# GpSimd's product waits for the LSTM's h of its slot, and the scan's step moves up to stand directly behind the LSTM's step

## The reference

```
def step(h, inp):                  # Mamba
    h = dA * h + d_t[..., None] * b_t[:, None, :] * u_t[..., None]
    y = jnp.einsum('bds,bs->bd', h, c_t)
def step(carry, xg_t):             # LSTM
    g = xg_t + h @ W_hh.T
    c = sigmoid(f) * c + sigmoid(i) * tanh(gg)
    h = sigmoid(o) * tanh(c)
```

## Time and profile before

| | |
|---|---|
| median of 3 runs | 3049.94 us (3046.9 to 3051.22) |
| the profiled execution: time, span | 3049.58 us, 3047.8 us |
| mean granted TensorE clock | 0.829 |
| busy: TensorE, VectorE, ScalarE, GpSimd | 82%, 62%, 45%, 33% |
| scans, weighings, products of drive in all | 256 each |

### The profile page before, as it was taken

One profiled execution on the slowest core, in us unless ns is written; L12 is line 12 of the kernel. 1 busy time (PEld: TensorE's weight loads), 2 busy tenths in 40 slices (PEclk: granted clock), 3 DMA queues, 4 the chain that ended last, 5 costly groups with the idle time before them and its releaser, 6 DMA issues.

```text
span 3047.8 us, 31113 instructions
## 1 busy us (share of the span) xinstructions
PE 2512.8 (82%) x7376; PEld 1272.4 (42%) x7376; DVE 1891.7 (62%) x6562; ACT 1384.6 (45%) x4624; POOL 1014.8 (33%) x913
## 2 busy tenths in 40 slices
PE   5677864489987999799978999699979996899698
PEld 1223442254444444444434444444444445444444
DVE  5575885467766777577756876677755555444322
ACT  3323333345544554455544554455534444444233
POOL 4343464135432564244523653245520002000200
PEclk8797556579995999689987999699968996898589
DMA  3232331023220332122311321123201210121021
GB/s 121 84 85 72 114 101 39 0 59 100 73 84 16 103 101 67 29 82 80 108 46 44 106 82 60 37 73 111 80 12 65 69 56 11 42 70 56 6 81 59
DMA packets 111776, 204.74 MB, mean 67 GB/s; under 512 B 14799, under 2 KB 24422, under 8 KB 111592
## 3 DMA queue, kind: packets, MB, share of 16 engines
q1 hardware_dynamic: 111592, 202.75, 22.1%
HBM read 195.36 MB, written 7.34 MB: 67 GB/s over the span
## 4 chain that ended last, share of the span: by engine, by line
PE 41%; DVE 32%; ACT 12%; issue 8%; POOL 1%; DVEq 0%; POOLq 0%; ACTq 0%
PE p_hid L651 9%; DVE state L1215 7%; PE p_turn L912 6%; ACT cell_t L926 4%; PE p_misc L668 4%; DVE cell L942 3%; DVE add_c L939 3%; DVE weighed L1224 3%; PE p_acc L668 3%; DVE p_turn L936 2%; DVE terms L828 2%; PE p_gate L465 2%; DVE hist L947 2%; PE p_hid L962 2%; PE p_up L469 1%
## 5 line engine op out<-in xcount | busy, mean ns | idle before, releaser
L912 PEld LDWEIGHTS p_turn<-hist,w_hh 22*128 22x128 f32 x2048 | 366.6, 222 | 1027.6 <-DVE hist L947 887.9
L912 PE MATMUL p_turn<-hist,w_hh 22*128 22x4 f32 x2048 | 452.2, 289 | 344.7 <-DVE hist L947 327.1
L651 PE MATMUL p_hid<-xhat,w 128*128 128x512 f32 x1024 | 580.9, 650 | 8.0 <-DVE xhat L381 7.2
L926 ACT ACTIVATE cell_t<-cell 20x4 f32<-20x4 f32 x1024 | 207.7, 203 | 679.8 <-DVE cell L942 679.8
L1142 POOL TENSOR_TENSOR drive<-du,rows 128x512 f32<-128x512 f32 x256 | 453.9, 1773 | 66.8 <-DVE p_turn L1215 28.5
L712 ACT ACTIVATE hid<-p_hid,b1f 128x512 f32<-128x512 f32 x512 | 351.8, 687 | 262.8 <-PE p_misc L668 141.2
L936 DVE SCALAR_TENSOR_TENSOR p_turn<-p_turn,cell 20x4 f32<-20x4 f32 x1024 | 170.7, 167 | 459.3 <-ACT p_turn L922 435.7
L388 POOL TENSOR_TENSOR n_rstd<-n_var,minus_half 128x4 f32<-128x4 f32 x56 | 61.7, 1103 | 1076.1 <-DVE n_var L376 1076.1
L1161 POOL TENSOR_TENSOR y<-y,weighed 128x512 f32<-128x512 f32 x192 | 242.4, 1263 | 411.1 <-DVE weighed L1224 410.4
L947 DVE SCALAR_TENSOR_TENSOR hist<-p_turn,cell_t 20x4 f32<-20x4 f32 x1024 | 162.6, 159 | 275.6 <-ACT cell_t L926 275.6
L922 ACT ACTIVATE p_turn<-p_turn 96x4 f32<-96x4 f32 x1024 | 157.9, 154 | 374.1 <-PE p_turn L912 371.3
(11 more groups left out here) (220 smaller groups left out, 3404.3 us busy)
## 6 DMA issues: line engine op xcount, KB each, us to landing
rows<-rows_dram SPq DMA_DIRECT2D x128, 512.0 KB, 5.1
w<-w_dram SPq DMA_DIRECT2D x128, 256.0 KB, 2.7
w<-in_w2T SPq DMA_DIRECT2D x128, 256.0 KB, 2.7
comb_b<-comb_dram SPq DMA_DIRECT2D x64, 512.0 KB, 4.6
rows<-comb_dram SPq DMA_DIRECT2D x128, 128.0 KB, 2.9
w<-in_w1T SPq DMA_DIRECT2D x16, 256.0 KB, 2.7
w_dram<-w SPq DMA_DIRECT2D x16, 256.0 KB, 2.1
out_xT<-result SPq DMA_DIRECT2D x8, 256.0 KB, 2.5
```

The lines of the kernel that those rows point to most:

```text
L651: nc.tensor.matmul(p_hid[:, v % 2, :], w1[:, v // FB, (v % FB) * P:(v % FB + 1) * P], xhat[:, :], start=True, stop=True).then_inc(g_h, 1)
L912: nc.tensor.matmul(gate_bank(i)[:, :, t:t + 1], w_hh[:, :], before, start=False, stop=False, skip_group_check=True).then_inc(gates_done, 1)
L926: nc.scalar.activation(cell_t[64:64 + PE_, :], cell[32:32 + PE_, :], ACT.Tanh, scale=0.5).then_inc(cell_tanh, 1)
```

## The change

`put_drive` gets an argument `step`. Where it is not zero, GpSimd waits before the product until h of the slot in which the product stands has been written. In `period` the scan's step (with the bursts of decays that go with it in period 0) is taken from the end of the slot and put behind the LSTM's step, ahead of `layer1`, `layer0`, `fold` and `soft`, on all engines. Which slots move the scan on is the same. Products outside a period (in `opening`) and the first product of a chunk (at the end of `soft`) keep `step` 0.

```
-    def put_drive(u, k):
+    def put_drive(u, k, step=0):
...
         if n >= 2:
             pool.wait_ge(scan_done, n - 1)
+        if step:
+            pool.wait_ge(h_done, step)
         nc.gpsimd.tensor_tensor(flat(drive[:, n % 2, :, :]), du[:, j, :], rows[:, (u * S + s_) % ROWS, 0, :], ALU.mult).then_inc(driven, 1)
...
+    step_now = {"h": 0}
...
-                put_drive(u, k + 1)
+                put_drive(u, k + 1, step_now["h"])
...
             next(lstm, None)
+            step_now["h"] = i * CH + slot + 1 if i < NCH and slot < CH else 0
...
+            wide = 0
+            heavy = layer1 is not None and slot >= att and 6 <= o < LAYER - 1 and slot < tail
+            if u < NCH and heavy and soft[1] > SOFT:
+                advance(scan, "scan", SCAN)
+            if u < NCH and layer1 is None and soft[1] > SOFT:
+                if done["scan"] == 0:
+                    for _ in range(6):
+                        next(burst, None)
+                elif done["scan"] % 2 == 0:
+                    next(burst, None)
+                if done["scan"] <= SCAN:
+                    advance(scan, "scan", SCAN)
             if layer1:
                 next(layer1, None)
-            wide = 0
-            heavy = layer1 is not None and slot >= att and 6 <= o < LAYER - 1 and slot < tail
...
-                elif layer1 is None:
-                    if done["scan"] == 0:
-                        for _ in range(6):
-                            next(burst, None)
-                    elif done["scan"] % 2 == 0:
-                        next(burst, None)
-                    if done["scan"] <= SCAN:
-                        advance(scan, "scan", SCAN)
-                elif heavy:
-                    advance(scan, "scan", SCAN)
```

## The result

| | before | after |
|---|---|---|
| median (lowest to highest), 4 runs each on one chip | 3050.58 us (3046.9 to 3051.95) | 3017.8 us (3012.74 to 3025.97) |
| the profiled execution: time, span | 3049.58, 3047.8 | 3012.74, 3010.9 |
| mean granted TensorE clock | 0.829 | 0.831 |

A forecast was written before the change was run, and what follows sets the result against it. The LSTM chain from h to h was taken as the bound, set by TensorE in heavy slots without a scan and DVE with one. Gains of 30 (periods 1 to 5) plus 3 (period 0) gave 3016.5 us, range 3003 to 3035.

The forecast's parts named there:

- the main term: Periods 1 to 5: 160 scans fall from 1.429 to 1.22 us, 33 us, less 3 for three late scans.
- the 0.37 us gap: Unexplained DVE idle time before three scans, letting the product in first; these stay late, 3 x 1.0 = 3 us.
- The margin of the race: Scan slots: scan starts 0.19 us after h, the waiting product 0.24, so the scan leads by 0.05.
- rival A: Scan slots: the product wins against the scan, slots about 3.23 us, +123 us, about 3173; chance 0.08.
- the hidden heads: Early part of scan (0.15 us) and product (0.19) before each asks for its inputs, putting the product about 0.09 behind.
- In a weighing slot DVE's sum stays: Weighing slots: weighing of 0.68 us with L841 or L828 after it instead of ahead, DVE's total unchanged.
- Rival B: Handovers cost: addition to y overlaps the next scan, or product's tail delays the weighing; 3023.5 to 3036; chance 0.15 for 3027 to 3042.
- Period 0: Scans gain 8 us, L1344 meeting the addition to y gives back 6; gain taken as 3, between loss 4 and gain 11.
- the clock: A changed granted TensorE clock, listed among the signs that the forecast was wrong; no size given.
- C: Counted delays are replaced one for one, for instance in light slots between layers; 3050 us; chance 0.03.
- D: Period 0 gives its 11 us and light slots gain from the product that left; 3005 or less; chance 0.04.

The follow-up runs named there:

- e1: Kernel before plus only GpSimd's wait for h ahead of the product, slot order as before: 3034.65 us, ratio 0.994.
- e2: Kernel before plus only the new order, scan's step moved ahead, without the wait for h: 3073.99 us, ratio 1.0075.
- e8: Kernel after plus a one-column DVE copy from PSUM partition 0 ahead of the weighing in `terms` slots, periods 1 to 5: 3034.71 us.
- e10: Kernel after plus 10 one-column DVE writes to an unused tile in the first LSTM step of period 6: 3030.52 us.
- e11: Kernel after plus 40 one-column DVE writes to an unused tile in the first LSTM step of period 6: 3037.93 us.
- e7: Kernel after, but in period 0 weighing steps go back behind `layer0` and `fold`, scan steps staying in front: 3020.96 us, ratio 0.9916.
- e6: Kernel after with period 0 put back to the old order and no wait: 3019.12 us, ratio 0.9913.
- after: The changed kernel itself, as first measured against the kernel before: 3017.8 us, ratio 0.9898.
- e3: The kernel after run once more, unchanged, against the kernel before: 3018.56 us, ratio 0.9879.
- e9: Kernel after, but only DVE's queue has the new order, other engines the old one: 3035.81 us, ratio 0.9945.
- e5: The ladder: kernel after plus small DVE writes before each scan, none in periods 0 and 1, up to four in period 5: 3115.81 us.

## Why the prediction was right, and where it was not

**The cause and the main term were right.** The scan was long because of GpSimd's operation ahead of it, either the product (slots of 3.2) or the addition to y (1.39). The sum put this at 33 us less 3; the scans gave 29.9 and the scan slots 32.1. Scan slots are 2.25, but for three of 3.51 behind the 0.37 us gap, exactly as many as were taken out of the sum. `e1` and `e2` show that both parts are needed: by the medians, alone they give -15 and +24 us, and in the scan slots of periods 1 to 5 alone -11 and +14, together -32.

**The margin of the race was mis-sized, harmlessly.** I took 0.08 us from DVE's end to GpSimd's start, from the weighing and the addition to y. From the end of L947 to the waiting product it is 0.16 to 0.17 (1331.59 + 0.16, 1331.91). The product was to start 0.24 behind its L947 and starts 0.33 behind it. The margin is 0.13 to 0.14, not 0.05, so rival A was further off than I thought. On the other hand the hidden heads on which I leaned are no protection: the ladder turns when the starts are equal. Had the signal taken 0.08, the scan would by the ladder still have won, with 0.05 to spare and no more.

**"In a weighing slot DVE's sum stays" is the step that failed.** Two DVE operations do not take the same time in both orders. `terms` behind the weighing begins 0.03 after its end, and the weighing behind `terms` began 0.08 before its end (the slot of before shown above). That is 0.11 to 0.12 a slot, in 60 `terms` slots 7 us, most of the 9 that weighing slots lost. `e8` shows the cause. The order in the earlier trace rows held the overlap (1346.92 + 0.69 against 1347.53), so a term for "who overlaps whom" could have been read there; for `terms` in the second place no row showed it.

**Rival B in its own form did not come.** The addition to y reaches 0.10 into the scan (forecast 0.05) and the product 0.03 into the weighing (1331.91 + 2.15, against 1334.03); the scan takes 1.23 and the weighing 0.69. Those hundredths are all that this overlap costs. (The 3036 that rival B names for all of its losses together does not come out of its own terms: 3016.5 + 7 + 8 + 3 is 3034.5.)

**Period 0 had, on average, the wrong sign.** Forecast -3; measured +1.6 to +4.9 between the two profiles of each kernel, and +2.4 between the means of all profiles with the same code in this stage, whose ranges overlap slightly (316.6 to 320.0 against 314.7 to 316.9). In the groups by line above the scans gave 7.5 of the forecast 8, and L1344 and L548 together took 6.5 where 6 were forecast (2.0 and 4.5). What the sum left out is the same 0.11 as with `terms`: in 20 slots L558 or L563 now begins 0.03 behind the end of a scan or a weighing, where that scan or weighing used to begin 0.08 ahead of their end. That is 2 us, and I had counted a gain in just those slots. How the rest divides is not measured.

**The total was right partly by luck.** In the profiles of the first table, against a forecast of -33 stand -26 to -27 in periods 1 to 5, +2 to +5 in period 0, -8 to -10 in periods 6 and 7 and -1 to -6 in the opening. Without the last two the kernel would be faster by some 21 to 25 us. With `e10` and `e11` counted, whose code in periods 1 to 5 is the same, the gain there is 20 to 27. What the last two stages gave is not the work of the change as such: `e7` and `e10` carry the change in periods 1 to 5, and their periods 6 and 7 took 590.8 and 590.7, as long as in the kernel before. `e6`, which has the change in periods 1 to 5 alone, was 25 us faster than the kernel before beside it, where `after` and `e3` were 33 and 31. Whether such lengths go with the kernel or with the execution is not settled; `e9` shows one kernel in two groups 19 us apart, and the kernel before ranged from 3037.7 to 3065.4 over 15 executions on one chip. The 0.2% (6 us) that the opening of this document names is therefore too little for comparing single executions. My prediction had the clock only as something that could make it wrong. That the 4 us of the light slots in periods 1 to 5 come from the product that left them is not shown either: these slots sum to 881.7 in the kernel after and to 888.0 and 888.6 in `e10` and `e11`, with the same code.

Rivals C and D did not come either: the delays were not replaced one for one, and period 0 gave nothing.

None of the variants is faster than the kernel after by more than the measurement can tell.

## What to carry to other kernels

Two engines that read the same memory and start nearly together need a fixed order: look for the one on the critical path whose mean is above its undisturbed time, and make the other wait for the event that lets the first one start; an earlier order without that wait made this kernel slower. When the order of two operations on one engine changes, compare the start of the second with the end of the first in both orders; the sum of the durations is not enough. Before a gain or loss is put down to a change, divide the span into stages, and see whether stages with the same code moved as well. And read in the trace what an edit really did before building on it: ten small writes meant as a pause of 1 us took 0.17.

## What the runs showed of the hardware that was not expected

- The race for the inputs turns within about 0.02 us: scan 0.01 ahead of the product, 1.22 to 1.23 us in 30 of 30; 0.01 behind, 2.33 in 26 of 26 (`e5`). The one that loses still hides 0.15 to 0.2 of its own time.
- From DVE's end to GpSimd's start a signal took 0.16 to 0.17 us behind the 20 x 4 operation L947, but 0.08 behind the 128 x 512 weighing. What makes the difference is not shown.
- One small DVE read of PSUM partition 0 ahead of the weighing brings `terms` forward by 0.11 us, from 0.03 after the weighing's end to 0.08 before it (`e8`).
- Mixture layers of period 7 with the same code took 49.1 us at a granted clock of 1.00 and 54.6 at 0.87, and nine executions of one kernel fell into two groups 19 us apart, with a mean granted clock of 0.831 to 0.834 and of 0.825 (`e9`).
- Ten writes of 128 x 1 by DVE, one behind the other, took 0.17 us together, and forty 0.72 (`e10`, `e11`).
